# A two-layer decoder on one core: the first stage rewritten (order of loads, of normalising, of products and of the writes of their parts)

## The chip, the cores and the metric

The kernel runs on one core of one Trainium2 chip. Its time is device microseconds of one execution; of the kernel before three were taken: 1434.57 (the median), 1432.37 and 1434.85.

## The reference

The input `x` has 2 sequences of 1024 tokens of 256 values; a context has 2 x 154 rows of 192. Six blocks follow one another, each with a layer norm ahead of it and a residual add behind it; all arithmetic is to fp32's accuracy.

```python
x = x + _L0_attn_ref(_layernorm(x, axis=-1), L0_attn_Wqkv, L0_attn_bqkv, L0_attn_Wout, L0_attn_bout)
x = x + _L0_xattn_ref(_layernorm(x, axis=-1), ctx_768, ...)
x = x + _L0_ffn_ref(...)        # gated, 8 experts
x = x + _L1_attn_ref(...)       # quantised gated recurrence
x = x + _L1_xattn_ref(...)
x = x + _L1_ffn_ref(...)        # 8 experts of 1024, two a token

def _L0_attn_ref(x, Wqkv, bqkv, Wout, bout):      # 16 heads of 16
    qkv = jnp.einsum('bsd,hde->bhse', x, Wqkv) + bqkv[None, :, None, :]
    q, k, v = jnp.split(qkv, 3, axis=-1)
    score = jnp.einsum('bhsd,bhtd->bhst', q, k)   # causal, softmax, times v, times Wout
```

The change touches the beginning alone: the first layer norm and the products that make q, k and v.

## The kernel before, in words

The function `front` is the kernel's first block of instructions; each of the five engines and the DMA queue of SyncE (SP) has its own list there and runs it in order, and waits only where it waits for a semaphore. The next block, the self-attention (`SelfAttention.run`), starts on every engine when all engines have come to the end of `front`.

The 2048 tokens are 16 tiles of 128, in four groups `g` of four tiles. For each group VectorE takes mean and variance (`moments`, lines 419 to 428), ACT takes the root, VectorE inverts it and makes a shift (`invert`), and ACT normalises the four tiles (`normalise`, line 383). TensorE (PE) turns them by eight transposes into two PSUM banks (`turn`, line 338), and ACT and VectorE copy one bank each to `xt` (`copy_xt`). The context is turned in the same way ahead of the last group.

Then come 16 products for q and k (line 367): a block `m` of 128 columns (q low, k low, q high, k high) times a group, all four groups of one block before the next block. Each product is a sum of two matmuls over 128 rows, and each matmul of fp32 is two passes in the trace, so a product is four passes of 512 columns. A product goes through a chain of three engines that splits it into three bf16 parts: ACT evicts it twice, as `full` and as its high part (lines 412, 414); VectorE subtracts (`rest`, line 467); POOL rounds that to the middle part (line 335); VectorE subtracts again (`lows`, line 444). The parts of a block go to a buffer `part` that has room for two blocks, SP writes them to DRAM as `scr_q` and `scr_k` (`write`, line 286), and ACT waits at the first product of blocks 2 and 3 until block 0 or 1 has been written (line 411). Behind the products come 16 for v, one for each tile (line 377, four passes of 256 columns), which VectorE evicts with a bias (line 475).

SP's list is: tokens of groups 0 and 1, the weights `w` (two DMAs), tokens of groups 2 and 3, the context, 16 small DMAs of bias; then, when their parts are there, the writes of blocks 0 and 1, a wait until these have landed, `attention.stage(sp, 0)` (18 loads of q and k rows for the first unit of self-attention, lines 519 and 524), and the writes of blocks 2 and 3. ACT's list begins with 17 DMAs of bias. POOL makes the identity, waits for the weights, copies their columns for q and k apart (line 311), makes masks, and fills `v_all` and rows 96 to 127 of the three slots of `sa_k` (lines 326 to 331) before its first middle part.

In self-attention PE multiplies q and k (line 753), VectorE takes row maxima (line 851); these go through POOL and PE and, by three DMAs on SP's queue (line 681), as extra rows into `sa_q`, and only then the products for the softmax begin (line 780). SP starts this block with 18 loads for unit 1. `o_tok`, the output, is the same memory as the normalised tokens `xn`.

Of the kernel before, what the change touches and what calls it, by code (L numbers as in the profile page):

```python
# [5 lines left out]
ALU = mybir.AluOpType  # L6
# [223 lines left out]
def front(c, ct, v_all, scr_q, scr_k, attention):  # L230
# [3 lines left out]
    wqkv, bqkv = c.arg["L0_attn_Wqkv"], c.arg["L0_attn_bqkv"]  # L234
    G = NT // 4
    with ExitStack() as ctx:
        def sb(name, shape, dt=F32):
            return c.sb(ctx, "fr_" + name, shape, dt)
        raw_ctx = sb("ctx", [MH, 4, DC])
        w, w_qk = sb("w", [P, KD, H, 3 * DH]), sb("w_qk", [P, 2, KD, D])  # L240
        bias, bias_v = sb("b_qk", [P, 2, KD]), sb("b_v", [P, H, DH])
        stats, mv = sb("stats", [P, NT, 6]), sb("mv", [P, NT, 2])
        ve, sd, rstd, shift = (sb(k, [P, NT]) for k in ("ve", "sd", "rstd", "shift"))
        xn, xt = attention.o_tok, sb("xt", [P, KD, N])
# [3 lines left out]
        w_in, b_sp, b_act, c_in, const, cast, w_set, v_zero = (  # L248
            c.sig("fr_" + k) for k in ("w_in", "b_sp", "b_act", "c_in", "const", "cast", "w_set", "v_zero"))
        measured, averaged, eps_in, rooted, inverted, shifted, normal, turned, c_turned, c_set, xt_act, xt_dve = (  # L250
            c.sig("fr_" + k) for k in ("measured", "averaged", "eps_in", "rooted", "inverted", "shifted", "normal",
                                       "turned", "c_turned", "c_set", "xt_act", "xt_dve"))
# [5 lines left out]
        steps = [(m, g) for m in range(len(blocks)) for g in range(NC)]  # L258
        NS = len(steps)

        def piece(n, p):
            m, g = steps[n]
            return part[:, m % 2, p, 512 * g:512 * g + 512]

        def load_bias(eng, i, done):
            for h in range(H):
                eng.dma_start(bias[DH * (h % 8):DH * (h % 8) + DH, i, h // 8:h // 8 + 1],
                              bqkv[h:h + 1, DH * i:DH * i + DH].rearrange("a b -> b a")).then_inc(done.sem, 16)

        with nc.Block() as block:  # L270
            @block.sync
            def _(sp):
                def tokens(g):
                    sp.dma_start(c.x[:, 4 * g:4 * g + 4, :],
                                 c.arg["x"].rearrange("b (t p) d -> p (b t) d", p=P)[:, 4 * g:4 * g + 4, :]
                                 ).then_inc(x_in[g].sem, 16)
                tokens(0)
                tokens(1)
                for k in range(KD):
                    sp.dma_start(w[:, k, :, :], wqkv.rearrange("h (k p) e -> k p h e", p=P)[k]).then_inc(w_in.sem, 16)  # L280
                tokens(2)
                tokens(3)
                sp.dma_start(raw_ctx[:, :, :], c.arg["ctx_768"].rearrange("b (i m) d -> m (b i) d", m=MH)).then_inc(c_in.sem, 16)
                load_bias(sp, 0, b_sp)

                def write(m):
                    i, mb = blocks[m]
                    sp.wait_ge(s_mid.sem, s_mid.at(NC * (m + 1)))
                    sp.wait_ge(s_low.sem, s_low.at(NC * (m + 1)))
                    for p in range(PARTS):  # L290
                        sp.dma_start((scr_q, scr_k)[i][p, P * mb:P * mb + P, :],
                                     part[:, m % 2, p, :]).then_inc(sent.sem, 16)
                write(0)
                write(1)
                sp.wait_ge(sent.sem, sent.at(16 * PARTS * 2))
                attention.stage(sp, 0)
                write(2)
                write(3)

            @block.gpsimd  # L300
            def _(pool):
# [5 lines left out]
                pool.wait_ge(link.sem, link.next())  # L307
                pool.wait_ge(w_in.sem, w_in.at(16 * KD))
# [17 lines left out]
                pool.memset(v_all[:, :, :, DH:VW], 0.0).then_inc(v_zero.sem, 1)  # L326
                pool.wait_ge(v_zero.sem, v_zero.at(1))
                pool.memset(v_all[:, :, :, DH:DH + 1], 1.0).then_inc(v_zero.sem, 1)
                pool.wait_ge(v_zero.sem, v_zero.at(2))
                for i in range(attention.SLOTS):  # L330
                    pool.memset(attention.k_st[96:P, i, :, :], 1.0).then_inc(attention.made.sem, 1)
                pool.wait_ge(attention.made.sem, attention.made.at(attention.SLOTS))
# [5 lines left out]
            def _(pe):  # L338
                def turn(g):
                    pe.wait_ge(normal.sem, normal.at(4 * g + 4))  # L340
# [5 lines left out]

                pe.wait_ge(const.sem, const.at(2))
                turn(0)
                turn(1)
                turn(2)  # L350
                pe.wait_ge(c_in.sem, c_in.at(16))
                for k in range(2):
                    for j in range(4):
                        last = pe.transpose(ps[0:96, 6 + k, MH * j:MH * j + MH], raw_ctx[:, j, 96 * k:96 * k + 96],
                                            c.ident[0:MH, 0:MH])
                last.then_inc(c_turned.sem, 1)
                pe.wait_ge(c_set.sem, c_set.at(1))
                turn(3)
                pe.wait_ge(w_set.sem, w_set.at(2 * KD))
                for n, (m, g) in enumerate(steps):  # L360
# [4 lines left out]
                    if n >= 8:  # L365
                        pe.wait_ge(s_high.sem, s_high.at(n - 7))
# [3795 lines left out]
```

## Time and profile before

| what | time before |
|---|---|
| median of three executions | 1434.57 us |
| the profiled execution | 1431.64 us |
| its span, from first to last instruction | 1429.9 us |
| PE busy | 1292.3 us, 90% |
| VectorE (DVE) busy | 1018.1 us, 71% |
| ACT busy | 881.4 us, 62% |
| POOL busy | 464.3 us, 32% |
| mean granted clock of PE | 0.952 |
| first q or k product (line 368) | 26.45 us |
| first matmul of self-attention (line 753) | 71.70 us |

Times in rows are microseconds from the span's start. A timeline row has start, length, engine, line, operation, what it writes and reads, and how many it merges; in brackets stands the engine's idle time ahead of it and what ended it. PEld is PE's weight load; a q behind an engine's name (SPq, ACTq) is its queue of DMA issues, and the length is that of issuing. PE's matmuls overlap, so the step from one start to the next is what one costs.

### The profile page before, as it was taken

To read this page: it belongs to the slowest core of one execution; us is meant where nothing else is said; L and a number is where in the kernel's file an instruction comes from. 1 tells how busy PE (TensorE), PEld (TensorE's weight loads), DVE (VectorE), ACT (ScalarE), POOL (GpSimd) and SP (SyncE) were. 2 spreads that over 40 slices of the span, in tenths; PEclk is the share of its full clock that TensorE was granted. 3 is DMA by queue.
4 is the path that set the end of the run, shared out by engine and by line. 5 is a ranking of instruction groups with operands and counts; after the bars stand their busy time and mean duration, and the time that the engine had idled before them with its cause. 6 is when DMAs were issued, how large, how long until landed. Compare 5 with 4: busy or idle time off the path is not lost. (4 is left out here: it accounts for less than half of the span.)

```text
span 1429.9 us, 27681 instructions
## 1 busy us (share of the span) xinstructions
PE 1292.3 (90%) x9691; PEld 1033.1 (72%) x9691; DVE 1018.1 (71%) x2017; ACT 881.4 (62%) x2216; POOL 464.3 (32%) x628
## 2 busy tenths in 40 slices
PE   5979999999699999999999766699988699999997
PEld 3534444436599999987888544578877699999995
DVE  4687877834666666567667896578866688888773
ACT  4426666684566666664210566478873688888883
POOL 5312222228443333334000556211100244444430
PEclk9999999999899999999999886699997799999998
DMA  4666323200000000021000400132203577777755
GB/s 91 210 101 160 46 46 51 43 2 5 31 1 2 1 2 2 1 71 56 1 1 1 98 1 1 23 74 46 49 1 127 168 233 231 233 232 233 231 156 188
DMA packets 97916, 116.15 MB, mean 81 GB/s; under 512 B 23549, under 2 KB 83187, under 8 KB 97779
## 3 DMA queue, kind: packets, MB, share of 16 engines
q1 hardware_dynamic: 88323, 99.83, 25.9%
q0 software_dynamic: 4416, 12.06, 2.6%
q10 hardware_dynamic: 5040, 2.49, 0.7%
q8 instruction: 78, 1.28, 0.4%
q14 instruction: 59, 0.48, 0.1%
HBM read 88.47 MB, written 16.55 MB: 73 GB/s over the span
## 5 line engine op out<-in xcount | busy, mean ns | idle before, releaser
L827 ACT ACTIVATE sa_probs<-ps 128x512 f32<-128x512 f32 (+1 forms) x304 | 154.3, 579 | 84.3 <-PE ps L780 83.2
L851 DVE TENSOR_REDUCE sa_top<-ps 128x2 f32<-128x1024 f32 (+3 forms) x160 | 171.4, 1114 | 37.8 <-PE ps L756 24.2
L2672 PE MATMUL ps<-me_h,me_w_parts 128*128 128x256 f32 x1104 | 140.4, 287 | 4.9 <-issue 3.0
L2672 PEld LDWEIGHTS ps<-me_h,me_w_parts 128*128 128x128 f32 x1104 | 137.0, 193 | 6.4 <-issue 3.2
L2686 PE MATMUL ps<-me_w_parts,me_mid 128*128 128x256 f32 x1104 | 136.6, 284 | 0.0
L2686 PEld LDWEIGHTS ps<-me_w_parts,me_mid 128*128 128x128 f32 x1104 | 132.7, 189 | 0.0
L3285 ACT ACTIVATE room<-ps,cx_top 128x154 f32<-128x154 f32 x256 | 96.5, 390 | 34.9 <-DVE cx_top L3341 34.4
L2753 DVE TENSOR_TENSOR me_w_parts<-me_chunk,me_w_parts 128x1024 fp32r<-128x1024 f32 x92 | 110.6, 1224 | 10.1 <-ACT me_w_parts L2713 8.5
L2737 ACT ACTIVATE me_full<-ps,me_b 128x256 f32<-128x256 f32 x184 | 94.7, 515 | 34.9 <-PE ps L2672 34.9
L2783 DVE TENSOR_TENSOR me_mid<-me_full,me_mid 128x256 fp32r<-128x256 f32 x184 | 89.1, 502 | 35.5 <-ACT me_mid L2739 34.8
L3159 POOL TENSOR_TENSOR room<-room 128x512 f32<-128x512 f32 x64 | 67.0, 1048 | 141.0 <-DVE room L3349 140.9
L2631 POOL DMA_INDIRECT moe_results<-me_result,mp_target x46 | 53.0, 1153 | 154.8 <-DVE me_result L2771 148.4
L753 PE MATMUL ps<-sa_k,sa_q 96*128 96x512 bf16 (+3 forms) x384 | 96.4, 335 | 5.7 <-DVE sa_top L851 4.2
L2713 ACT ACTIVATE me_w_parts<-me_chunk 128x1024 fp32r<-128x1024 f32 x92 | 99.9, 1146 | 0.0
L2739 ACT ACTIVATE me_mid<-ps,me_b 128x256 fp32r<-128x256 f32 x184 | 95.9, 521 | 0.0
L3341 DVE TENSOR_REDUCE cx_top<-ps 128x2 f32<-128x308 f32 x128 | 59.7, 470 | 47.9 <-PE ps L3201 47.7
L1440 PE MATMUL ps<-f_w_high,f_hid 128*128 128x512 f32 (+1 forms) x320 | 91.0, 369 | 2.5 <-DVE x L1581 2.5
L780 PE MATMUL ps<-sa_q,sa_k 99*128 99x512 bf16 (+3 forms) x384 | 88.3, 329 | 0.7 <-ACT sa_probs L827 0.4
L3201 PE MATMUL ps<-hd_keys,cx_qh 128*128 128x308 f32 x256 | 83.5, 340 | 0.4 <-DVE cx_ql L3334 0.3
L3963 ACT ACTIVATE cn_p<-ps,cn_top 128x154 f32<-128x154 f32 x256 | 79.0, 409 | 7.5 <-DVE cn_top L4017 7.3
L794 PE MATMUL ps<-sa_probs,v_all 128*32 128x512 f32 (+3 forms) x768 | 81.6, 498 | 1.8 <-ACT sa_o_raw L834 1.1
L753 PEld LDWEIGHTS ps<-sa_k,sa_q 96*128 96x128 bf16 x384 | 34.4, 99 | 62.3 <-DVE sa_top L851 33.2
(465 smaller groups left out, 3283.6 us busy)
## 6 DMA issues: line engine op xcount, KB each, us to landing
me_chunk<-in_L_ffn_W_dram SPq DMA_DIRECT2D x92, 512.0 KB, 4.3
sa_k<-scr_k SPq DMA_DIRECT2D x48, 128.0 KB, 4.4
sa_q<-scr_q SPq DMA_DIRECT2D x96, 64.0 KB, 4.4
cn_qd<-cn_qh SPq DMA_DIRECT2D x60, 64.0 KB, 2.0
scr_q<-room SPq DMA_DIRECT2D x6, 512.0 KB, 5.0
scr_k<-room SPq DMA_DIRECT2D x6, 512.0 KB, 5.1
me_b<-in_L_ffn_b_dram SPq DMA_DIRECT2D x23, 128.0 KB, 3.9
x<-in_x_dram SPq DMA_DIRECT2D x4, 512.0 KB, 5.9
```

Of the source, the lines that this page charges most:

```text
L753: last = pe.matmul(out[:, a:a + w], self.q_st[0:96, slot, half, h0 + j, q0:q0 + P], self.k_st[0:96, slot, h0 + j, k0:k0 + w], start=True, ...
L827: act.activation(probs[:, step % self.PROBS, h0:h0 + many, 0:w], src[:, :, 0:w], ACT.Exp, scale=DH ** -0.5).then_inc(exped.sem, 1)
L851: dve.tensor_reduce(top2[:, k % 2, k0 // 512, h0:h0 + many, sb % HBLK], src[:, :, 0:w], AX.X, ALU.max).then_inc(freed.sem, 1)
L1440: last = pe.matmul(ps[:, O_BANK + n % RING, 0:w], hid[:, g % 2, net, m, part, cols], wt[:, m, w0:w0 + w], start=(i == 0), stop=(i == len(t ...
L2672: last = pe.matmul(ps[:, MID + n % 4, 0:RT], w[:, u % 2, 0, i, DM * k + P * b:DM * k + P * b + P], h[:, u % 2, j, k, :], start=(m == 0), s ...
L2686: last = pe.matmul(ps[:, OUT + n % 2, 0:D], mid[:, u % 2, b, i, P * a:P * a + P], w[:, u % 2, 1, j, D * b:D * b + D], start=(m == 0), stop ...
L2713: act.activation(part(n, 0), chunk[:, n % BUF, :], ACT.Copy).then_inc(w_high.sem, 1)
L2737: act.activation(full[:, n % 4, :], ps[:, MID + n % 4, 0:RT], ACT.Relu, bias=col).then_inc(s_full.sem, 1)
L2739: act.activation(mid[:, u % 2, b, 0, :], ps[:, MID + n % 4, 0:RT], ACT.Relu, bias=col).then_inc(high.sem, 1)
L2753: dve.tensor_tensor(part(n, 1), chunk[:, n % BUF, :], raw(part(n, 0)), ALU.subtract).then_inc(w_low.sem, 1)
L2783: dve.tensor_tensor(mid[:, u % 2, b, 1, :], full[:, n % 4, :], raw(mid[:, u % 2, b, 0, :]), ALU.subtract).then_inc(low.sem, 1)
L3285: last = act.activation(p[:, h + i, :], ps[:, S_BANK + n % SR, M * i:M * i + M], ACT.Exp, bias=top[:, t % 2, h + i:h + i + 1], accum_out=d ...
```

## The change

All of it is in `front`, but for one wait in self-attention.

- Loads: tokens come as tiles 0 and 1, tiles 2 and 3, then the weights, then groups 1, 2, 3. The 32 column DMAs of the q and k bias become two DMAs of rows on ACT's queue, which PE turns with one transpose; the v bias goes to the end of SP's loads.
- Root table: ACT takes a root of a one as its first work.
- Normalising: VectorE takes tiles 0 and 1 of group 0 and all four of group 1; POOL the first tile of groups 2 and 3; ACT the rest.
- PE: 16 products of the identity with itself, into a bank that is not read, stand ahead of the first turn. Turns of groups 1, 2, 3 stand behind products 0, 2 and 4. Products go in pairs of blocks, group by group (q low and k low of group 0, of group 1, ...). The context's transposes stand behind the fourth v product, in the same ring of banks, and ACT copies them.
- Parts: four buffers, one for each block, and no wait of ACT for a write; the fourth is in memory of `xn` that self-attention writes later, so VectorE waits there for all writes ahead of its first output. SP writes two blocks when both are done.
- POOL fills `v_all` ahead of the weights; `sa_k`'s first slot is filled by VectorE at the very start, the others copied from it by ACT at the end of its list.

```diff
-        part = attention.weights.room[:, 4096:10240].bitcast(BF16).rearrange("p (i a n) -> p i a n", i=2, a=PARTS)
+        part = [attention.weights.room[:, 4096 + 3072 * m:7168 + 3072 * m].bitcast(BF16).rearrange(
+            "p (a n) -> p a n", a=PARTS) for m in range(3)]
+        part.append(attention.weights.room[:, 0:3072].bitcast(BF16).rearrange("p (a n) -> p a n", a=PARTS))
...
-        steps = [(m, g) for m in range(len(blocks)) for g in range(NC)]
+        steps = [(m, g) for pair in (0, 2) for g in range(NC) for m in (pair, pair + 1)]
+        ring = [("value", u) for u in range(NT)]
+        ring[4:4] = [("context", k) for k in range(2)]
...
+        def normal(eng, t, done):
+            eng.tensor_scalar(xn[:, t, :], c.x[:, t, :], mv[:, t, 0:1], rstd[:, t:t + 1],
+                              ALU.subtract, ALU.mult).then_inc(done.sem, 1)
...
-                tokens(0)
-                tokens(1)
+                tokens(0, 2, x_first)
+                tokens(2, 4, x_in[0])
                 for k in range(KD):
                     sp.dma_start(w[:, k, :, :], wqkv.rearrange("h (k p) e -> k p h e", p=P)[k]).then_inc(w_in.sem, 16)
-                tokens(2)
-                tokens(3)
+                tokens(4, 8, x_in[1])
+                tokens(8, 12, x_in[2])
+                tokens(12, 16, x_in[3])
                 sp.dma_start(raw_ctx[:, :, :], ...).then_inc(c_in.sem, 16)
-                load_bias(sp, 0, b_sp)
+                sp.dma_start(bias_v[:, :, :], bqkv[:, 2 * DH:3 * DH].partition_broadcast(P)).then_inc(bv_in.sem, 16)
...
-                write(0)
-                write(1)
-                sp.wait_ge(sent.sem, sent.at(16 * PARTS * 2))
-                attention.stage(sp, 0)
-                write(2)
-                write(3)
+                for pair in (0, 2):
+                    n = NS // 2 * (1 + pair // 2)
+                    sp.wait_ge(s_high.sem, s_high.at(n))
+                    sp.wait_ge(s_mid.sem, s_mid.at(n))
+                    sp.wait_ge(s_low.sem, s_low.at(n))
+                    write(pair)
+                    write(pair + 1)
+                    if pair == 0:
+                        sp.wait_ge(sent.sem, sent.at(16 * PARTS * 2))
+                        attention.stage(sp, 0)
...
 # POOL, behind the weight copies
+                for g in (2, 3):
+                    pool.wait_ge(inverted.sem, inverted.at(g + 1))
+                    normal(pool, 4 * g, normal_pool)
...
 # PE
+                for i in range(16):
+                    pe.matmul(ps[:, 6, 0:P], c.ident[:, :], c.ident[:, :], start=True, stop=True)
+                pe.wait_ge(b_in.sem, b_in.at(32))
+                pe.transpose(ps[:, 7, 0:2 * KD], bias_rows[:, :], c.ident[0:2 * KD, 0:2 * KD]).then_inc(b_turned.sem, 1)
+                turn(0)
+                for n in range(NS):
+                    if n < 2:
+                        pe.wait_ge(w_set.sem, w_set.at(KD * (n + 1)))
+                    product(n)
+                    if n in (0, 2, 4):
+                        turn(n // 2 + 1)
...
 # ACT
-                    if m >= 2 and g == 0:
-                        act.wait_ge(sent.sem, sent.at(16 * PARTS * (m - 1)))
...
+                act.wait_ge(warm.sem, warm.at(1))
+                act.activation(one[:, 1:2], one[:, 0:1], ACT.Sqrt).then_inc(warm.sem, 1)
+                root(0)
+                normalise(0)
+                root(1)
+                copy_xt(0)
+                (the bias from PSUM)
+                copy_xt(1)
+                root(2)
+                normalise(2)
+                evict(0)
+                root(3)
+                normalise(3)
+                evict(1)
+                copy_xt(2)
+                evict(2)
+                evict(3)
+                copy_xt(3)
+                for n in range(4, NS):
+                    evict(n)
+                (two copies of the context, then two of the fill of sa_k)
...
 # VectorE
+                dve.memset(one[:, :], 1.0).then_inc(warm.sem, 1)
+                dve.memset(attention.k_st[96:P, 0, :, :], 1.0).then_inc(attention.made.sem, 1)
                 moments(0)
                 invert(0)
+                normal(dve, 0, normal_dve)
+                normal(dve, 1, normal_dve)
+                moments(1)
+                invert(1)
+                copy_xt(0)
+                for t in range(4, 8):
+                    normal(dve, t, normal_dve)
+                moments(2)
+                invert(2)
+                copy_xt(1)
+                moments(3)
+                invert(3)
                 (identb; then the rest and the lows of each product)
+                    if n in (1, 3):
+                        copy_xt((n + 3) // 2)
...
 # VectorE, in self-attention, ahead of the first output
+                        else:
+                            dve.wait_ge(self.sent.sem, self.sent.at(16 * PARTS * 2 * KD))
```

## Rows read from the trace of the kernel before

**Rows 1.** Timeline of PE and its weight loads, first 72 us.
```profile
20.47 1.97 PE L343 MATMUL ps<-ident,room 128*128 128x128 f32 x8 [2.86 <-ACT room L388]
...
26.45 29.23 PE L368 MATMUL ps<-fr_xt,fr_w_qk 128*128 128x512 f32 x64
...
28.16 0.34 PEld L368 LDWEIGHTS ps<-fr_xt,fr_w_qk 128*128 128x128 f32 x1 [0.52 <-issue]
...
29.01 0.34 PEld L368 LDWEIGHTS ps<-fr_xt,fr_w_qk 128*128 128x128 f32 x1 [0.52 <-issue]
...
30.20 0.19 PEld L368 LDWEIGHTS ps<-fr_xt,fr_w_qk 128*128 128x128 f32 x1 [0.24 <-issue]
...
30.63 0.19 PEld L368 LDWEIGHTS ps<-fr_xt,fr_w_qk 128*128 128x128 f32 x1 [0.24 <-issue]
...
63.75 7.17 PE L377 MATMUL ps<-fr_w,fr_xt 128*128 128x256 f32 x32 [1.16 <-DVE v_all L475]
...
71.70 0.22 PE L753 MATMUL ps<-sa_k,sa_q 96*128 96x128 bf16 x1 [0.78 <-PEq L270]
```

**Rows 2.** Timeline of ACT and its DMA issues.
```profile
0.81 7.64 ACTq L267 DMA_DIRECT2D fr_b_qk<-in_L_attn_bqkv_dram  x16
...
8.96 1.28 ACT L385 ACT_TABLE_LOAD   x1 [8.96 <-issue]
...
18.35 2.07 ACT L388 ACTIVATE room<-x,fr_shift,fr_rstd 128x256 f32<-128x256 f32 x4 [0.44 <-DVE fr_shift L435]
...
46.76 0.69 ACT L412 ACTIVATE fr_full<-ps,fr_b_qk 128x512 f32<-128x512 f32 x1 [3.51 <-DMA scr_q<-room]
...
47.91 0.69 ACT L412 ACTIVATE fr_full<-ps,fr_b_qk 128x512 f32<-128x512 f32 x1
```

**Rows 3.** Timeline of VectorE (DVE).
```profile
5.03 1.41 DVE L422 BATCH_NORM_STATS2 fr_stats<-x 128x6 f32<-128x256 f32 x4 [5.03 <-DMA x<-in_x_dram]
...
10.92 1.40 DVE L422 BATCH_NORM_STATS2 fr_stats<-x 128x6 f32<-128x256 f32 x4
...
13.39 1.40 DVE L422 BATCH_NORM_STATS2 fr_stats<-x 128x6 f32<-128x256 f32 x4
...
15.11 2.56 DVE L427 TENSOR_SCALAR fr_ve<-fr_mv 128x4 f32<-128x4 f32 x1
...
26.69 0.69 DVE L440 COPY fr_xt<-ps 128x512 f32<-128x512 f32 x1 [1.79 <-PE ps L343]
```

**Rows 4.** Timeline of POOL.
```profile
11.15 1.42 POOL L311 COPY fr_w_qk<-fr_w 128x256 f32<-128x256 f32 x4 [9.60 <-DMA fr_w<-in_L_attn_Wqkv_dram]
...
14.13 3.51 POOL L326 MEMSET v_all<- 128x4096 f32 x1
```

**Rows 5.** Timeline of SyncE's DMA issues: writes, loads, writes.
```profile
39.58 3.44 SPq L291 DMA_DIRECT2D scr_q<-room  x3
...
54.58 2.67 SPq L519 DMA_DIRECT2D sa_k<-scr_k  x6
...
62.97 1.62 SPq L291 DMA_DIRECT2D scr_q<-room  x3
...
64.69 3.46 SPq L291 DMA_DIRECT2D scr_k<-room  x3
```

**Rows 6.** Windows around the clock's fall: stretch, length, busy time by engine, clock, DMA.
```profile
77.40:80.86 3.46, 1.50 (x9) 0.44 (x8) 3.36 (x4) 0.00 (x0) 1.11 (x5) 1.00 1.12 174
...
80.86:87.69 6.83, 6.48 (x27) 2.79 (x25) 5.41 (x5) 1.22 (x3) 0.00 (x0) 0.50 0.61 106
```

**Rows 7.** Groups by line and shape: count, busy us, mean ns, idle before.
```profile
L3529 POOL TENSOR_SCALAR cn_xn<-x,x_mv,cn_rstd 128x256 f32<-128x256 f32 x4 | 4.8, 1212 | 0.0
...
L2713 ACT ACTIVATE me_w_parts<-me_chunk 128x1024 fp32r<-128x1024 f32 x92 | 99.9, 1146 | 0.0
```

**Rows 8.** Timeline of self-attention's start: the rows of maxima and their first use.
```profile
80.79 2.92 SPq L681 DMA_DIRECT2D sa_q<-sa_neg  x3
...
85.80 1.49 PE L780 MATMUL ps<-sa_q,sa_k 99*128 99x512 bf16 x3
```

More of the change, by code:

```diff
@@ L233, in front @@
     nc, ps = c.nc, c.ps
-    wqkv, bqkv = c.arg["L0_attn_Wqkv"], c.arg["L0_attn_bqkv"]
     G = NT // 4
@@ L247, in front @@
         x_in = [c.sig(f"fr_x_in{g}") for g in range(G)]
[L248 to L252, printed above, removed]
+        x_first = c.sig("fr_x_first")
@@ new lines, in front @@
+        w_in, w_set, b_in, b_turned, b_set, bv_in, c_in, c_set, const, cast, v_zero = (
+            c.sig("fr_" + k) for k in ("w_in", "w_set", "b_in", "b_turned", "b_set", "bv_in", "c_in", "c_set", "const", "cast",
+                                       "v_zero"))
+        warm, measured, averaged, eps_in, rooted, inverted, shifted = (
+            c.sig("fr_" + k) for k in ("warm", "measured", "averaged", "eps_in", "rooted", "inverted", "shifted"))
+        normal_act, normal_dve, normal_pool, turned, xt_act, xt_dve = (
+            c.sig("fr_" + k) for k in ("normal_act", "normal_dve", "normal_pool", "turned", "xt_act", "xt_dve"))
@@ L325, in _ @@
                 pool.wait_ge(link.sem, link.next())
[L326 to L332, printed above, removed]
                 for n in range(NS):
@@ L345, in turn, with product @@
                         last.then_inc(turned.sem, 1)
[L347 to L360, printed above, removed]
+                def product(n):
+                    m, g = steps[n]
                     i, mb = blocks[m]
-                    if n < NC:
-                        pe.wait_ge(xt_act.sem, xt_act.at(n + 1))
-                        pe.wait_ge(xt_dve.sem, xt_dve.at(n + 1))
-                    if n >= 8:
+                    if n < 8:
+                        pe.wait_ge(xt_act.sem, xt_act.at(g + 1))
+                        pe.wait_ge(xt_dve.sem, xt_dve.at(g + 1))
+                    else:
                         pe.wait_ge(s_high.sem, s_high.at(n - 7))
@@ L383, in normalise, with root @@
                 def normalise(g):
+                    act.wait_ge(shifted.sem, shifted.at(g + 1))
+                    for t in range(4 * g + (2 if g == 0 else 1), 4 * g + 4):
+                        act.activation(xn[:, t, :], c.x[:, t, :], ACT.Identity, bias=shift[:, t:t + 1],
+                                       scale=rstd[:, t:t + 1]).then_inc(normal_act.sem, 1)
+                def root(g):
                     act.wait_ge(eps_in.sem, eps_in.at(g + 1))
                     act.activation(sd[:, 4 * g:4 * g + 4], ve[:, 4 * g:4 * g + 4], ACT.Sqrt).then_inc(rooted.sem, 1)
-                    act.wait_ge(shifted.sem, shifted.at(g + 1))
-                    for t in range(4 * g, 4 * g + 4):
-                        act.activation(xn[:, t, :], c.x[:, t, :], ACT.Identity, bias=shift[:, t:t + 1],
-                                       scale=rstd[:, t:t + 1]).then_inc(normal.sem, 1)
                 def copy_xt(g):
```

124 lines of the change are left out of this document (70 added, 54 removed).

## The prediction

> **What bounds the kernel now.** The chain of waits names nothing of this stage, since its lines are those of the expert stage at the end; so I read the page's shares first (the table above: PE 90%, every other engine at 71% or less) and then the timelines of the first 72 us, engine by engine. The reader is to see three things. First, PE has its first product at 26.45 and its last value product ends at 63.75 + 7.17 = 70.92; from 26.45 on it idles once, 1.16 us [rows 1]. So what the stage costs is when the products start, plus the products themselves. Second, the start is late for four reasons. ACT issues bias DMAs from 0.81 to 8.45 and one more, loads its table at 8.96, and only then takes the first root, although the tokens were there at 5.03 [rows 2, 3]. VectorE's small add at 15.11 takes 2.56 us and ends at 17.67, just when POOL's memset of 14.13 + 3.51 ends [rows 3, 4]; a second one waits likewise. All four groups are turned, and the context too, ahead of the first product. Third, the wait for the parts that the change removes (ACT's 3.51 us at 46.76) is on ACT, not on PE: PE's products run through it [rows 1, 2]. Its only price is the 1.16 us at 63.75, when the value evictions come late. The next stage starts at 71.70 [rows 1], 0.78 after the last value product.
>
> **The clock.** Product passes start 0.85 us apart at 28.16 and 29.01 and 0.43 apart at 30.20 and 30.63 [rows 1]: 1.2 GHz, then 2.4 GHz. The granted clock has no record ahead of that change, so the spacing decides. It rose within 3.8 us of the start of the unbroken products at 26.45, and fell at 80.86 after 3.46 us of which PE was busy for 1.50 [rows 6].
>
> **The change, step by step.** *Start of the products.* ACT now issues two bias DMAs (about 0.48 each, from 7.64 / 16) and loads its table while nothing has landed. But the tokens of group 1 now come behind the weights, and VectorE's copy of the first turned group, which the first product needs, stands in its queue behind the moments of group 1. The bytes ahead are the same 1.79 MB that had landed when POOL took the weights at 11.15 [rows 4], so group 1 lands at about 11.0 (9.5 if the weights alone were slow; at the latest 13.4, when the third group was there before [rows 3]). From the first statistics to the next work is 13.39 - 10.92 = 2.47; a copy is 0.69 [rows 3]. First product: 11.0 + 2.5 + 0.7 = 14.2 instead of 26.45.
>
> *What that hides.* Group 0 (statistics from 5.03 for 1.41, small work and root 1.1, two tiles each on VectorE and ACT 1.0) is normalised by 8.6 [rows 2, 3]. The 16 identity products are 32 passes from about 2. At a transpose's 0.22 (1.97 for eight, less the last one's tail) they end at 9.1 and group 0 is turned by 11; at the 0.34 of a weight load at 12.9 and 14.9 [rows 1]. I take 0.22, nearest in columns; the other would cost 1.4. VectorE's memset of 32x4096 has no row. POOL's kind takes 3.51 [rows 4], and VectorE waits 3.4 us for group 1, so between 0 and 1.3 us; I take 0. The weight copies (1.42 after about 9.4) end before 14.2. POOL's memset of v_all now lies ahead of the weights, and no small add meets it. ACT's two copies of the fill stand behind the context copies, at about 54.8 by the sum below. By 0.52 for 256 columns and 1.15 for 1024 [rows 2, 7], 4096 take 3.7: both end at 62.1, under VectorE's end; in proportion to 0.69 for 512 they take 5.5 and end at 65.8, 1.4 later. I take the first.
>
> *From the first product to the fifth.* The first runs at 1.2 GHz: 4 x 0.85 = 3.4, to 17.6. Then comes a chain through ACT, which holds normalising and evicting in one queue: half a turn 0.8 (18.4), copy 0.6, root and wait 0.65, three tiles 1.5 (21.2), eviction 1.15 (47.91 - 46.76), root and wait 0.65, three tiles 1.5, eviction 1.15 (25.7), then on VectorE a rest, a low and the copy of group 2, each a pass over 512 columns like the copy's 0.69 (27.8) [rows 2, 3]. POOL's two tiles of 1.2 [rows 7] and its masks may hold the low for 0.2. PE has done four products and three turns by 24.8, so it idles about 3.2 and takes the fifth at 28.0.
>
> *To the end.* Twelve products of 4 x 0.43 = 20.5; the last turn at full rate 0.9; eight context transposes 0.5; sixteen values of 0.87 (7.17 for eight, less the tail) 13.9: 35.8, ends 63.8. With the 0.78 the next stage starts at 64.6, not 71.7.
>
> *SyncE.* Both blocks of a pair are now written together. Nine products and the ninth's eviction, rest and low end at 40.3. Three writes took 39.58 to 46.65 [rows 2, 5]; three more at the 1.15 at which SyncE was held per write (3.46 / 3) make 10.5: 50.8. The eighteen loads took 54.58 to 62.97, 8.4: 59.2. Six writes' issue took 62.97 to 68.15, 5.2: 64.4 [rows 5]. SyncE, which had 3 us to spare before, now ends with VectorE: start at 64.7, a gain of 7.0.
>
> *After the block.* The last writes land about 10.5 after their first issue: 1.8 us into the next stage before, 5.0 now. The loads of the next unit and the rows of the maxima (issued 80.79, first used 85.80 [rows 8]) queue behind them: between 0 and 3.2 us; I take 0.7, since five microseconds lie between issue and use and a load needs about 3. The new wait on VectorE ahead of the first output is for writes that are in at 70, long before it; what would queue behind it is every later maximum. It costs 0.
>
> *Sum.* -7.1 (PE) + 0.1 (SyncE) + 0.7 = -6.3. The profiled execution took 1431.64 (span 1429.9), so 1425.3; the median of the runs is 1434.57, 2.93 above it, so 1428.3.
>
> **A rule against it.** The clock fell after a stretch of little work [rows 6]. The Trainium skill (TensorE: Matmul & The Clock Gate, "What's actually happening") says that the half rate is the default, that only sustained activity lifts it and that idleness brings it back. By that rule the identity products warm an array that then waits from 11 to 14.2 and is cold again; the trace agrees as far as the fall at 80.86 goes, and the sum is the one above; without the rule it is the first rival's.
> The small add that ended with POOL's memset is what the Trainium skill (GPSIMD Engine Reference, "1. Specifications") leads one to expect: POOL shares its SBUF interfaces with VectorE. By it POOL's two tiles could hold VectorE's cast of the identity for up to 1.2, beside ACT's eviction, so the sum stays.
>
> **Rivals.** (1) PE is still at 2.4 GHz at 14.2. For it: 32 passes just before. Against: 3.2 us of idleness. The first product takes 1.7 and the chain moves up by about 1.9: 1426.4. (2) The 3.2 us ahead of the fifth product let the clock fall once more. The one fall in the rows lasted 6.8 us [rows 6], which at half rate costs 3.4, a shorter one half of that: about 1431. Against: PE is busy without a break for ten microseconds before. (3) The DMA queue sets the pace: the whole 3.2 is paid for the rows: 1430.8. For it: SyncE's spare time is gone. Against: five microseconds of room. (4) Slower: the clock never settles in the products, because turns, the wait at the fifth and the evictions break them up. Each microsecond at 1.2 GHz costs half a one; the gain of 6.3 is gone if the half rate lasts 12.6 us past 28.0, and if it lasts to the last product, 20.5 of work more is paid: 1434.6 + 14 = 1449; with the half rate up to 45, about 1437. Against: before, it rose within 3.8 us of unbroken products. (5) The change does nothing for the time: it would need something else to end at 71.7; only SyncE's writes could, at 17.5 us instead of 10.5. I see no row for it.
>
> **How the numbers follow.** Forecast 0.46, its own range 1426.5 to 1430.0 (9.5 instead of 11.0 for group 1 is worth about 1; the bounds on the products and the memset 1.3 to 1.4 the other way); (1) 0.12; (2) 0.20; (3) 0.13; (4) 0.05; (5) 0.04. The range 1425.5 to 1432.0 takes in (1) to (3) but for the tail of (2). Within 0.2% (2.9 us, what a measurement of this kernel can tell from no change) lie a third of (2), part of (3) and (5): 0.13; slower is (4): 0.05; faster 0.82.
>
> **What would show it.** First product near 14.2, at passes 0.85 apart, released by VectorE's copy of group 0; group 1's statistics released by a DMA near 11; PE idle about 3 us ahead of the fifth product, released by VectorE's copy of group 2; no idle of ACT on the parts; the next stage's first matmul near 64.7, with SyncE's last write issued just before. I am wrong if the first product is after 17, if PE's passes are 0.85 apart after 30, if the next stage starts after 68, or if the first use of the rows falls more than 16 us into that stage instead of 14.1.

## The result, and the profile after

The forecast was wrong in its sign: the changed kernel is slower.

| | kernel before | changed kernel |
|---|---|---|
| median, us (runs) | 1433.74 (11) | 1441.16 (11) |
| lowest to highest, us | 1430.1 to 1436.32 | 1434.38 to 1444.34 |
| profiled execution: span, mean granted clock | 1429.9, 0.952 | 1439.3, 0.943 |
| ratio | | 1.0048, 95% interval 1.0034 to 1.0062 |

That is 6.9 us slower (1433.74 x 0.0048), where 6.3 us faster had been forecast. The stage that was rewritten does end earlier. The loss arises 580 us later, in a stage whose code is the same in both kernels.

**The first stage.** PE's timeline of the changed kernel answers to [rows 1] (start us, length us, engine, line, operation, out<-in, shape, count, idle before and its releaser):
```profile
1.61 6.09 PE L379 MATMUL ps<-ident 128*128 128x128 f32 x32 [1.61 <-POOL ident L315]
...
9.16 1.06 PE L360 MATMUL ps<-ident,room 128*128 128x128 f32 x8 [1.31 <-ACT room L413]
13.23 3.63 PE L373 MATMUL ps<-fr_xt,fr_w_qk 128*128 128x512 f32 x4 [3.00 <-DVE fr_xt L497]
...
21.91 1.88 PE L373 MATMUL ps<-fr_xt,fr_w_qk 128*128 128x512 f32 x4
27.65 3.75 PE L373 MATMUL ps<-fr_xt,fr_w_qk 128*128 128x512 f32 x4 [3.86 <-DVE fr_xt L497]
31.19 1.91 PE L360 MATMUL ps<-ident,room 128*128 128x128 f32 x8
32.90 19.44 PE L373 MATMUL ps<-fr_xt,fr_w_qk 128*128 128x512 f32 x44
...
56.16 10.57 PE L404 MATMUL ps<-fr_w,fr_xt 128*128 128x256 f32 x48
67.51 0.22 PE L817 MATMUL ps<-sa_k,sa_q 96*128 96x128 bf16 x1 [0.78 <-PEq L277]
```
The first product starts 13.22 us earlier (26.45 to 13.23), the next stage 4.19 earlier (71.70 to 67.51). The product at 27.65 takes 3.75 us where the one at 21.91 took 1.88: half rate. The windows say so too (stretch, length, busy time by engine, then clock, DMA share, GB/s; they answer to [rows 6]). The first is around the fifth product, the second the start of the next stage, the third and fourth come below:
```profile
26.80:33.63 6.83, 5.98 (x13) 3.45 (x14) 3.87 (x7) 1.87 (x4) 2.03 (x2) 0.50 0.00 0
77.98:88.22 10.24, 9.09 (x33) 3.97 (x32) 6.87 (x7) 3.81 (x8) 0.98 (x2) 0.50 0.85 171
649.83:653.77 3.94, 0.01 (x2) 0.00 (x1) 3.94 (x4) 1.12 (x2) 3.94 (x2) 1.00 0.56 111
654.85:658.26 3.41, 3.41 (x10) 2.63 (x9) 3.41 (x2) 0.13 (x1) 3.41 (x1) 0.51 0.00 0
```
VectorE's timeline answers to [rows 3]: group 1's statistics, and the copy of group 2 that the fifth product waits for.
```profile
9.94 1.41 DVE L479 BATCH_NORM_STATS2 fr_stats<-x 128x6 f32<-128x256 f32 x4 [1.40 <-DMA x<-in_x_dram]
...
26.82 0.68 DVE L497 COPY fr_xt<-ps 128x512 f32<-128x512 f32 x1
```
SyncE's issues answer to [rows 5]: the last writes, then the next stage's loads.
```profile
62.65 3.30 SPq L297 DMA_DIRECT2D scr_k<-room  x3
67.47 3.08 SPq L583 DMA_DIRECT2D sa_k<-scr_k  x6
```
**Where the time goes.** The same matmul was looked up in several traces, and its start compared with that in the profiled kernel before. Negative is earlier; the header gives the time in the kernel before. e2, e4, e9 and e10 are experiments below, and e2 is the kernel before up to 645.

| kernel | 71.7 | 105 | 345 | 645 | 655 | 900 | 1081 | 1415 |
|---|---|---|---|---|---|---|---|---|
| changed | -4.19 | -0.34 | 2.64 | 1.01 | 6.78 | 8.40 | 7.84 | 9.37 |
| e2 | 0.07 | 3.15 | 6.04 | 4.42 | 4.41 | 5.10 | 2.26 | 1.80 |
| e4 | -3.73 | 2.90 | 5.59 | 4.01 | 4.17 | 4.36 | 1.48 | 1.93 |
| e9 | -3.79 | -1.34 | 0.90 | 0.98 | 1.00 | 1.75 | 2.07 | 0.84 |
| e10 | -7.56 | -1.52 | -0.08 | -0.08 | -0.08 | 0.65 | -2.17 | -1.08 |

Read the first row alone, and the lead seems to be lost by 105 and 345. The granted clock was at half in the changed kernel for 10.2 us from 78.0, for 6.8 from 98.5 and for 6.8 from 327.2; in the kernel before only for 6.8 from 80.9. The second row corrects that: the kernel before, traced once more (e2), was at half for 10.2 us from 81.4, for 6.8 from 101.9 and for 6.8 from 330.6. The first trace of the kernel before is the exception: in all other traces of this study a fall begins between 92 and 102, and in all but e11 one between 325 and 331. One execution's clock falls are no property of a kernel. What no other row of the table has is the step of 5.8 us between 645 and 655.

There, in the dense feed-forward block of layer 0, GpSimd splits the output weights w2 into a high and a low part while VectorE splits the hidden rows. VectorE's timeline of the kernel before, then POOL's:
```profile
646.49 0.71 DVE L1558 TENSOR_TENSOR f_hid<-room,f_hid 128x512 fp32r<-128x512 f32 x1
647.12 1.28 DVE L1544 TENSOR_TENSOR hd_keys<-ps,hd_keys 128x512 fp32r<-128x512 f32 x2
```
```profile
644.54 2.11 POOL L1371 CAST f_w_high<-room 128x2304 fp32r<-128x2304 f32 x1 [8.18 <-DMA room<-_L_ffn_w_shared_out_dram]
646.73 5.50 POOL L1373 TENSOR_TENSOR f_w_low<-room,f_w_high 128x2304 fp32r<-128x2304 f32 x1
```
The same of the changed kernel, and PE's logits (L1461), which need VectorE's L1610, the line behind the held one:
```profile
647.50 5.02 DVE L1624 TENSOR_TENSOR f_hid<-room,f_hid 128x512 fp32r<-128x512 f32 x1
```
```profile
644.67 2.11 POOL L1437 CAST f_w_high<-room 128x2304 fp32r<-128x2304 f32 x1 [7.25 <-DMA room<-_L_ffn_w_shared_out_dram]
646.86 5.12 POOL L1439 TENSOR_TENSOR f_w_low<-room,f_w_high 128x2304 fp32r<-128x2304 f32 x1
```
```profile
653.77 0.73 PE L1461 MATMUL ps<-hd_wq,hd_keys 128*128 128x512 f32 x2 [3.94 <-DVE hd_keys L1610]
```
Before, VectorE's subtraction starts 0.24 us ahead of POOL's and takes 0.71. After, it starts 0.64 us behind and takes 5.02, until POOL's is done; the next in VectorE's queue is what the logits wait for, and PE idles 3.94 us at a clock of 1.00 and then works 3.41 us at half of it (the third and fourth window above). The idle time and half of the slow stretch make 5.6 of the 5.8 us. Below, this meeting of the two subtractions is called the collision. The kernel before is not spared a hold: its next two subtractions, from 650.09, start behind POOL's and take 5.21 us together where 0.7 each would be usual. But PE has its logits to do meanwhile and is busy throughout (4.00 us of the 4.00 from 650 on). What decides is which of VectorE's subtractions is caught. The Trainium skill (SBUF — State Buffer, "SBUF: two separate sides") says that VectorE with two SBUF inputs and a GpSimd operation that reads SBUF share a pair of ports, and that the first to start holds it for the whole instruction. The rows agree: VectorE's takes 0.71 us when it is first and 5.02 when POOL is; POOL's takes 5.50 behind VectorE and 5.12 when it is first.

Why is POOL early? Relative to SyncE's first issue of w2 (634.92, changed 635.96), VectorE's subtraction starts at +11.57 and +11.54: the same. The last part of w2 lands at +9.57 and +8.65: 0.9 us earlier in the changed kernel. The DMA queues in the 9 us from that issue, in the kernel before (packets, MB, share of the 16 engines):
```profile
q1 hardware_dynamic: 2679, 2.67, 88.0%
q8 instruction: 1, 0.02, 0.7%
q14 instruction: 1, 0.01, 0.2%
```
In the changed kernel the same stretch holds one queue, and the 6 us ahead of the issue the other two:
```profile
q1 hardware_dynamic: 2768, 2.75, 90.0%
```
```profile
q8 instruction: 1, 0.02, 1.0%
q14 instruction: 1, 0.01, 0.6%
```
The kernel before has a packet of instructions of queue 8 (16 KB, 0.96 us on its engine) among the weights; in the changed kernel it passed before they began. Queue 8 moves 78 such packets in each kernel. The changed kernel's trace holds 74 more instructions of TensorE and its sequencer (20197 against 20123), all of them ahead of this block, and 63 of them are the 16 identity products, so each packet would come earlier in the work if queue 8 carries TensorE's program. That was the theory to test; e5 and e6 bear it out.

### The profile page after: what moved, and what is told of

Same layout as the page of the kernel before. It is cut to its first block and busy times, and to the rows that moved or that the text cites. A ratio compares the mean times of both kernels' runs of the same rounds, so it can differ in the third digit from the quotient of the medians.

```text
span 1439.3 us, 27729 instructions
## 1 busy us (share of the span) xinstructions
PE 1305.8 (91%) x9724; PEld 1040.7 (72%) x9724; DVE 1024.6 (71%) x2024; ACT 887.2 (62%) x2214; POOL 456.4 (32%) x627
## 5 line engine op out<-in xcount | busy, mean ns | idle before, releaser
L2819 DVE TENSOR_TENSOR me_w_parts<-me_chunk,me_w_parts 128x1024 fp32r<-128x1024 f32 x92 | 110.4, 1222 | 10.2 <-ACT me_w_parts L2779 8.7
L817 PE MATMUL ps<-sa_k,sa_q 96*128 96x512 bf16 (+3 forms) x384 | 98.5, 340 | 5.2 <-DVE sa_top L915 3.6
```

The lines of the kernel that those rows point to most:

```text
L817: last = pe.matmul(out[:, a:a + w], self.q_st[0:96, slot, half, h0 + j, q0:q0 + P], self.k_st[0:96, slot, h0 + j, k0:k0 + w], start=True, ...
L2819: dve.tensor_tensor(part(n, 1), chunk[:, n % BUF, :], raw(part(n, 0)), ALU.subtract).then_inc(w_low.sem, 1)
```

## The experiments

Each ratio is to runs of the kernel before on the same chip, whose median was 1434.74 beside e1 to e4, 1434.37 beside e5 to e8 and 1433.67 beside e9 to e12.

**e1 and e2: the collision cut short, in both kernels**
```diff
-                    pool.tensor_tensor(w2_low[:, k, :], w2[:, k, :], raw(w2_high[:, k, :]), ALU.subtract
-                                       ).then_inc(w2_l.sem, 1)
+                    for c0 in range(0, (E8 + 1) * D, 576):
+                        last = pool.tensor_tensor(w2_low[:, k, c0:c0 + 576], ...)
+                    last.then_inc(w2_l.sem, 1)
```


> The changed kernel with GpSimd's two w2_low subtractions of the first feed-forward block each cut into four of 576 columns. In the changed kernel's trace one of them (5.12 us) stood in the way of VectorE's subtraction into hid, which took 5.02 us in place of 0.69; TensorE idled 3.94 us behind it, its clock fell, and the lead against the kernel before went from +1.03 to +8.2 us (late). Theory A (this collision is what makes the changed kernel slower, in nearly every run): no hold longer than about 1.4 us (5.12 / 4 = 1.28), no idle over 1 us ahead of the logits, and the time falls by 6 to 7 us, to about 1434.5 or a ratio to the kernel before near 1.000. Theory B (the collision is a hit of one execution, 0.24 us of margin either way, and the loss lies elsewhere, in clock falls of the stages behind the front): the time stays within 2 us of the changed kernel's, ratio 1.004 or 1.005.

> The kernel before with the same cut of the w2_low subtractions. In its trace the collision did not stop TensorE. Theory A (the kernel before escapes the collision in nearly every run): no change, ratio within 0.002 of 1. Theory B (both kernels hit it in some runs): a gain of one to three us, ratio 0.998 to 0.999, and a smaller spread.

Measured: e1 1435.41, ratio 0.9998 (0.9982 to 1.0014); e2 1434.58, 0.9996 (0.9981 to 1.0012). In e1 POOL is first again (649.14, VectorE 649.66), but the hold is 1.46 us and PE's idle 0.39. Theory A in both: the cut gives back about 7 us where the collision stops PE, nothing where it doesn't.

**e3: the next stage started later**
```diff
                     last.then_inc(mm.sem, 1)
+                pe.wait_ge(v_set.sem, v_set.at(9))
+                for i in range(5):
+                    pe.matmul(ps[:, (NS + NT + 2) % 8, :], xt[:, 0, 0:P], xt[:, 0, 0:512], start=True, stop=True)
```


> The changed kernel with five more matmuls of 128x512 at the end of its front, which nothing reads (4 passes each, 0.85 us each from the values' products: 4.3 us), so that the next stage starts near 71.8 us, where the kernel before starts it (71.70). Theory A (what is lost behind the front hangs on when the stages start against transfers that do not move with them): the stages then run as in the kernel before, and the time is not longer than the changed kernel's, 1438 or less. Theory B (each us of front is a us of the total, and the rest of the loss has nothing to do with the start): 4.3 us more than the changed kernel, about 1445.5, ratio 1.008.

Measured: 1441.91, 1.0053 (1.0034 to 1.0072), between the two numbers, so it decides little. The stage began at 69.45, not 71.8. Its trace has the collision again: POOL 647.80, VectorE 648.39 for 5.07 us, PE idle 3.98.

**e4: no identity products**
```diff
-                for i in range(16):
-                    pe.matmul(ps[:, 6, 0:P], c.ident[:, :], c.ident[:, :], start=True, stop=True)
```


> The changed kernel without its 16 identity products (1.61 to 7.70 us, 32 passes). If they only warm the first turns: group 0's turn at 9.16 runs at half rate (1.97 or more in place of 1.06) and the first product, released at 13.23 by VectorE's copy, starts about 0.9 later and at half rate as now; the fall of the clock at 26.8 to 33.7 stays, and the time rises by 1 us at the most, ratio to the kernel before 1.005. The rival: with no early work on TensorE the clock rises once, at the first products, and does not fall again at 26.8; then the front ends 2 to 3 us sooner and the ratio is 1.003.

Measured: 1433.47, 0.9987 (0.9971 to 1.0003): 8.7 us less than the changed kernel by the ratios (0.0061 x 1434). Both sides of the expectation were wrong on the time. The front did what the first side said: the clock is at half rate at the fifth product again (29.7 to 33.1), and the next stage starts at 67.97 where it was 67.51. The time falls all the same. The two traces agree in the front's end and part in the feed-forward block, where e4 has no collision (VectorE, then POOL):
```profile
650.50 0.97 DVE L1622 TENSOR_TENSOR f_hid<-room,f_hid 128x512 fp32r<-128x512 f32 x1
```
```profile
648.82 2.11 POOL L1435 CAST f_w_high<-room 128x2304 fp32r<-128x2304 f32 x1 [8.43 <-DMA room<-_L_ffn_w_shared_out_dram]
651.01 5.50 POOL L1437 TENSOR_TENSOR f_w_low<-room,f_w_high 128x2304 fp32r<-128x2304 f32 x1
```
VectorE is 0.51 us ahead again. This run pointed from the front's work to the number of its instructions.

**e5 and e6: the kernel before, with the products, and with nothing but instructions**
```diff
                 pe.wait_ge(const.sem, const.at(2))
+                for i in range(16):                                   # e5
+                    pe.matmul(ps[:, 7, 0:P], c.ident[:, :], c.ident[:, :], start=True, stop=True)
+                for i in range(126):                                  # e6
+                    pe.wait_ge(const.sem, const.at(2))
                 turn(0)
```


> The kernel before with the 16 identity products added at TensorE's start, where it idles, and nothing else: 63 more instructions in TensorE's stream. In the traces so far a 16 KB packet of the instruction queue 8 lies 5.1 to 5.5 us behind the first issue of the feed-forward weights in the kernel before and in the changed one without the 16 products, and the last of these weights lands 9.6 to 9.8 us behind that issue; in the three kernels with the 16 products the packet lies 4.5 to 4.7 us ahead of that issue, and the weights land after 8.7 to 8.8, so that GpSimd's subtraction starts 1 us earlier and catches VectorE. Theory A (the 63 instructions move the packet, the packet moves the landing): in this kernel too the packet lies ahead of the issue, the weights land after some 8.7 us, VectorE is held about 5 us, TensorE idles about 4 us, and the time rises by 6 to 8 us, ratio 1.004 to 1.006. Theory B (what the rest of the change does to the stages behind the front sets it): no hold, ratio within 0.002 of 1.

> The kernel before with waits that are already met, at the same place on TensorE: 63 more instructions, as in the run with the 16 products, and no matmul. Theory A (their number alone): the same rise as with the 16 products, 6 to 8 us, packet ahead of the issue, hold of 5 us. The rival within it (it is TensorE's early work, through its clock, that sets the later phases): no change, ratio within 0.002 of 1.

Measured: e5 1441.40, 1.0050 (1.0035 to 1.0065); e6 1443.25, 1.0065 (1.0048 to 1.0082). Waits that are already met, in 63 instructions run while TensorE has nothing to do, cost the kernel before 9 us. e6's queues in the 6 us ahead of the first issue of w2, and in the 9 us from it:
```profile
q8 instruction: 1, 0.02, 1.0%
```
```profile
q1 hardware_dynamic: 2683, 2.67, 89.7%
q14 instruction: 1, 0.01, 0.5%
```
The packet has moved from 5.45 us behind the issue (in the kernel before) to 3.67 ahead of it, nearly where it is in the changed kernel, and VectorE, POOL and PE meet as there, each from its timeline:
```profile
650.39 5.50 DVE L1560 TENSOR_TENSOR f_hid<-room,f_hid 128x512 fp32r<-128x512 f32 x1
```
```profile
650.24 5.10 POOL L1375 TENSOR_TENSOR f_w_low<-room,f_w_high 128x2304 fp32r<-128x2304 f32 x1
```
```profile
657.15 1.22 PE L1397 MATMUL ps<-hd_wq,hd_keys 128*128 128x512 f32 x2 [4.42 <-DVE hd_keys L1546]
```

The same move shortens a wait in the front. In the kernel before a packet of queue 8 lies at 40.71, among the first three writes of parts, and the last of these lands 7.07 us after the first issue (39.58 to 46.65). In e6 no packet of queue 8 lies there: it lands after 5.12, ACT waits 1.56 us for the parts where it waited 3.51, PE's 1.16 us of idleness among the values is gone, and the next stage starts 1.25 us earlier. The traces of e5 and e12 agree with e6 in this, that of e2 with the kernel before. So the 9.3 us are what is left after a gain in the front, and the wait that the change was made to remove hung in part on the place of a packet.

**e7: the same columns in 47 fewer instructions**
```diff
-                for i in range(16):
-                    pe.matmul(ps[:, 6, 0:P], c.ident[:, :], c.ident[:, :], start=True, stop=True)
+                pe.wait_ge(warm.sem, warm.at(1))
+                for i in range(4):
+                    pe.matmul(ps[:, 6, :], c.ident[:, :], ones[:, :], start=True, stop=True)
...
 # VectorE, as its first work
+                dve.memset(ones[:, :], 1.0)
```


> The changed kernel with 4 products of 512 columns (of ones) in place of the 16 of 128: the same columns on TensorE, 47 instructions fewer. Theory A: the packet comes later in the program and lies again behind the issue of the weights, by some 2 to 4 us, while these are under way; they land after more than 9.3 us, no hold, and the time is that of the kernel without the 16 products, ratio 0.998 to 1.000. Theory B (the early work costs the time): as the changed kernel, ratio 1.004 to 1.006.

Measured: 1433.31, 0.9987 (0.9970 to 1.0005): the time as theory A has it, its trace not. The packet lies 1.0 us behind the issue, where the transfers have hardly begun; w2 lands after 9.05, VectorE comes 0.26 us late (649.04 against 648.78) and is held 5.38. The twelve times spread from 1425.40 to 1440.93, the widest of the study; the profiled one, at 1440.93 (span 1439.2), is the longest. It may be that at this place the race falls either way; only the one execution has a trace, so that is not shown.

**e8 and e10: the front's own wait removed, without products and with the cut**
```diff
# ScalarE, e10 (e8: copy_xt(3) stays behind evict(3))
                 normalise(3)
-                evict(1)
                 copy_xt(2)
+                evict(1)
+                copy_xt(3)
                 evict(2)
                 evict(3)
-                copy_xt(3)
...
# VectorE, e10, right behind the rest of product n (e8: copy_xt(2) at n == 0, copy_xt(3) at n == 3)
+                    if n < 2:
+                        copy_xt(n + 2)
                     if n >= 1:
                         lows(n - 1)
-                    if n in (1, 3):
-                        copy_xt((n + 3) // 2)
```


> The changed kernel without the 16 products, with the subtractions of w2_low cut into four, and with the copies of token group 2's turned rows moved ahead: on ScalarE ahead of the second eviction, on VectorE right behind the first rest, so that the fifth product does not wait for VectorE's later work. In the run without the 16 products that product began at 29.39 after 3.62 us idle while its turn had ended at 24.06; with the copies at 24.3 to 25.8 it begins near 26, the next stage near 64.5 in place of 67.97. If the front's gain reaches the end (theory: only the collision ate it), the total falls by 3 us against that run and 5 against the kernel before, ratio 0.996 to 0.998. The rival (the first stage of attention gives the lead back, since there TensorE waits for VectorE and its clock falls): ratio 0.998 to 1.000.

> The kernel without the 16 products, with the cut subtractions and the early copies of group 2, and now also group 3's copies ahead: on ScalarE behind the second eviction, on VectorE behind the second rest. There the seventh product began at 31.55 after 2.26 us idle and its clock fell at 32.2; its turn had ended at 27.57. Now it begins near 29 with less than 1 us idle, without a fall, and the next stage starts near 62.5 in place of 65.83. If leads of the front reach the end: 2 to 3 us less than that run, ratio 0.996 to 0.997. If the first stage of attention gives them back: 0.998.

Measured: e8 1430.68, 0.9981 (0.9968 to 0.9993); e10 1429.57, 0.9965 (0.9952 to 0.9978). Both beat the kernel before and the changed one; e10 is the fastest, 5.0 us (0.35%) under the kernel before. In e8 the fifth product starts at once, but the seventh waits (31.55, 2.26 us idle, clock down at 32.2). In e10 no product waits behind the first, and from the second on they run at full rate, by their spacing (PE):
```profile
27.30 1.04 PE L360 MATMUL ps<-ident,room 128*128 128x128 f32 x8
28.17 19.05 PE L373 MATMUL ps<-fr_xt,fr_w_qk 128*128 128x512 f32 x44
...
53.69 8.90 PE L402 MATMUL ps<-fr_w,fr_xt 128*128 128x256 f32 x40 [0.71 <-DVE v_all L536]
64.14 0.22 PE L815 MATMUL ps<-sa_k,sa_q 96*128 96x128 bf16 x1 [1.55 <-PEq L277]
```
The next stage starts at 64.14, later than the 62.5 expected: the values now wait 0.71 us for VectorE, and the stage's first matmul comes 1.55 us after them where it was 0.78, since SyncE issues its last writes from 60.40 to 63.70, behind the last value product's end (62.59). Of the lead in the front (3.73 in e4, 5.88 in e8, 7.56 in e10) the ratios show 1.9, 2.7 and 5.0 us at the end: about half to two thirds. Where the rest goes was not separated from the clock falls of attention's start: the granted clock is at half there for 20.5 us at a stretch in e4 and e10 and for 10.2 in e8, where e2 has 10.2.

**e9: the same changed kernel, POOL told to wait**
```diff
                 pool.wait_ge(w2_in.sem, w2_in.at(16 * 2 * HB))
+                pool.wait_ge(rec.w_in.sem, rec.w_in.at(16 * rec.NW))
```


> The changed kernel, in which GpSimd waits ahead of its two rounds on w2 for four more transfers that are on their way anyway (they landed at 647.37 where w2 landed at 644.61). Nothing else is touched: the 16 products, the packet of instructions and the landing of w2 stay. If the order of two starts is all that costs the 6 to 8 us: GpSimd's first subtraction starts near 649.6, VectorE's subtraction at 647.5 goes through in about 0.7, TensorE does not idle ahead of the logits, the time falls by 6 to 8 us, ratio 0.999 to 1.001. If the landing or the packet costs in another way: as the changed kernel, 1.004 to 1.006.

Measured: 1433.52, 1.0001 (0.9989 to 1.0014). Packet (4.47 us ahead of the issue) and landing (+8.67) are those of the changed kernel; only the order of the two starts is turned round, and the 7 us are gone (VectorE, then POOL):
```profile
647.47 0.68 DVE L1625 TENSOR_TENSOR f_hid<-room,f_hid 128x512 fp32r<-128x512 f32 x1
```
```profile
650.20 5.18 POOL L1440 TENSOR_TENSOR f_w_low<-room,f_w_high 128x2304 fp32r<-128x2304 f32 x1
```

**e11 and e12: what 63 instructions cost with the collision cut.** e11 is e10 with the 126 waits, e12 is e6 with the cut of e1.

> The same kernel as the one beside it with both early copies, with 126 waits that are already met at TensorE's start: 63 more instructions, so that the packets of instructions lie where they lie in the changed kernel. With the subtractions cut into four, the earlier landing of w2 has nothing long to catch. If the collision is all that the place of the packets decides: within 0.0015 of the kernel beside it. If other stages hang on it too: 1 to 3 us slower.

> The kernel before with the 126 met waits, which cost it 8.9 us, and with the subtractions of w2_low cut into four. If the waits cost by the collision alone: back to the kernel before, ratio 0.999 to 1.001. If a part of the 8.9 us comes from elsewhere: that part stays, ratio 1.001 to 1.003.

Measured: e11 1430.85, 0.9984 (0.9971 to 0.9996), 0.0019 over e10; e12 1436.69, 1.0019 (1.0003 to 1.0035), 0.0046 under e6. So the collision is about 6.6 of e6's 9.3 us, and some 2.7 us come from elsewhere, although e12's next stage starts 1.6 us earlier (70.07). A part has a place: cross-attention of layer 1, where TensorE waits for rows that come back by DMA. PE in e4, and then in e12:
```profile
943.00 0.48 PE L3918 MATMUL ps<-cn_kd,cn_qd 96*128 96x308 f32 x2 [0.25 <-DMA cn_qd<-cn_ql]
```
```profile
943.99 0.48 PE L3858 MATMUL ps<-cn_kd,cn_qd 96*128 96x308 f32 x2 [1.35 <-DMA cn_qd<-cn_ql]
```
In e12 a packet of queue 8 lies at 941.84, within the transfer; in e4 none does between 934 and 947. All eight kernels traced with 63 more instructions or above idle 0.99 to 1.85 us there, and in each a packet of queue 8 lies 2.1 to 3.1 us ahead of that matmul; the six with at most 27 more idle 0.21 to 0.25, and none of them has a packet there. The rest, 1 to 2 us and what the front gains, is open.

The traces in one table; times are relative to the first issue of w2:

| kernel | TensorE's instructions in the trace, over before | queue 8's packet | last part of w2 lands | VectorE's start less POOL's |
|---|---|---|---|---|
| before, e2 | 0 | +5.45, +5.28 | 9.57, 9.68 | -0.24, -0.36 |
| e4, e8, e10 | 11 | +5.10, +5.05, +4.94 | 9.82, 9.77, 9.66 | -0.51, -0.45, -0.34 |
| e7 | 27 | +1.02 | 9.05 | +0.26 |
| e5, e6, e12 | 63 | -3.70, -3.67, -3.65 | 9.13, 9.16, 9.03 | +0.16, +0.15, +0.29 |
| changed, e1, e11 | 74 | -4.49, -4.47, -4.48 | 8.65, 8.79, 8.53 | +0.64, +0.52, +0.79 |
| e3 | 94 | -4.65 | 8.72 | +0.59 |

Where the packet lies well among the weights (+4.9 to +5.5), POOL comes second; at e7's +1.02 it comes first. The rows of 63 land 0.4 us later than those of 74. In them and in the kernel before a packet of queue 14 still lies among the weights, at +2.3 to +2.5; that it is the cause is not shown, for the kernel before, with both packets, lands no later than e4 with queue 8's alone.

## Why the prediction was wrong

**The step that failed** is "The 16 identity products are 32 passes from about 2", costed as passes that other work hides. The passes were sized nearly rightly: 0.19 us each where 0.22 had been taken, done at 7.70, hidden. What was left out is that they are 63 instructions, which move the packets of all later instructions. e6 prices that without a single pass: 9.3 us, 6.6 of them the collision. And the "Sum" closed with the block and its rows: everything behind was taken to run as before, only earlier. In the feed-forward block that rested on a margin of 0.24 us which the trace of before shows, between two rows that the prediction did not read. The changed kernel falls on the other side of it, by 0.64.

Its other steps, against the changed kernel's trace:

- *First product* 14.2 forecast, 13.23 measured, half rate, released by VectorE's copy: right. Group 1's tokens were there by 9.94, not 11.0; the lower bound of 9.5 had been named.
- *Group 0 turned* by 11 forecast, 10.2 measured. The memset on VectorE took 3.47 us and pushed the first statistics from 5.03 to 5.36 only.
- *Fifth product* 28.0 after 3.2 us idle forecast, 27.65 after 3.86 measured: right, through the chain that was named. POOL held VectorE's low by 0.50 us (25.83) where 0.2 had been allowed for.
- *Its clock*: the second rival was right. Four passes and a turn at half rate (3.75 and 1.91 in place of 1.88 and 1.04) cost 2.7, so the next stage starts at 67.51, not 64.7, and SyncE's last write, forecast to end at 64.4, is issued by 65.95. The forecast gain of 7.0 was 4.2, and the prediction's own sign for this, passes at half rate after 30, came.
- *The rows after the block*: first used 14.71 us into the next stage where it had been 14.1 [rows 8]: 0.6 for the 0.7 taken. Only half of it is a longer way from issue to use (76.93 to 82.22, 5.29 us, where it was 5.01); the rows are also issued 0.3 us later into the stage. So the size was right partly by luck.
```profile
82.22 0.61 PE L844 MATMUL ps<-sa_q,sa_k 99*128 99x512 bf16 x1 [0.92 <-DMA sa_q<-sa_neg]
```
- *The wait for the parts*, of which the prediction said that its only price is the 1.16 us: right for the trace that it read. In e6 both are smaller without the change, when all that was added is instructions.
- *The slower rival* had the right sign by a mechanism that did not occur: the clock was up from 33.7 on.
- With the collision alone removed (e9) the changed kernel is level with the kernel before, not 4 us ahead: the 2.7 us of instruction place of e12, if they weigh as much here, and a part of the front's lead that attention's start does not pass on. That last part is argued, not shown.

## What to carry to other kernels

Count instructions, not only their time: here 63 on TensorE, run where it idles, moved the later packets of queue 8 by 9 to 12 us against the transfers that they met, for worse in two places and for better in one. Before believing that a stage behind the change "runs as before", look in its trace for two starts within a microsecond on VectorE and GpSimd where one holds up the other, and fix their order by a wait or cut the longer operation; e9's one wait was worth 6.7 us (0.0047 x 1434), more than the front's lead of 4.2. And trace the kernel before twice: e2 stood 6 us from the first trace at 345, before any of its code differed.

## What the runs showed of the hardware

- A 16 KB packet of instructions among the loads of w2 (two transfers of 1024 KB and two of 128) makes its last part land about 1 us later (9.7 to 9.8 us in e4, e8 and e10 against 8.5 to 8.8 in the kernels with 74 more instructions or above; e10 and e11 differ in the 126 waits alone, 9.66 and 8.53). The Trainium skill (Runtime: NRT & Kernel Launch, "Instruction fetch mechanics") says that programs are fetched in blocks of 16 KiB and that crossing a boundary is mostly hidden. Here the wait that cost most was not for instructions but for VectorE (PE's 3.94 us), behind a transfer whose landing depends on the packet's place; whether TensorE also waits for instructions somewhere, no trace here shows.
- The late landing was worth about 7 us to the kernel before (6.6 by e6 and e12): a delay that kept two engines apart.
- With POOL's subtraction in pieces of 576 columns (1.42 to 1.88 us each) VectorE slips in between: its subtraction takes 1.46, 1.20 and 1.69 us in e1, e11 and e12, not 5.
